# Attention scores in two pairs of PSUM banks, read by one exponential per pair, and two banks instead of three for the max pass

## The chip, the core and the metric

The program runs on one core of one Trainium2 chip. The metric is the device time of one execution in microseconds, from the first to the last instruction; the median of several executions is compared. The core has five engines with queues of their own: TensorE (PE in the profile, with its weight loads as PEld), VectorE (DVE), ScalarE (ACT), GpSimd (POOL) and SyncE (SP, which here only issues DMAs). They meet through semaphores. PSUM, where TensorE writes its results, has eight banks of 512 fp32 values per partition.

## What is computed

A macaron transformer block over 8 sequences of 1024 tokens with 256 channels: half a mixture-of-experts feed-forward, attention, and another half of the same feed-forward. The change lies in the attention alone, with 16 heads of 16 channels.

```python
x = x + 0.5 * ffn(layernorm(x))          # 8 experts, each 1024 tokens at most
x = x + attention(layernorm(x))
x = x + 0.5 * ffn(layernorm(x))

def attention(x):                         # B, T, C = 8, 1024, 256; H, D = 16, 16
    q, k, v = rope(heads(Wq, bq)), rope(heads(Wk, bk)), heads(Wv, bv)
    att = einsum('bhqd,bhkd->bhqk', q, k) / sqrt(D)
    att = softmax(where(causal, att, NEG_BIG), axis=-1)
    return einsum('bhqk,bhkd->bhqd', att, v) @ Wp.T + bp
```

## The kernel before

Attention works in 32 groups, each four heads of one sequence. Every engine runs the same loop over the groups, three groups in one turn of a hardware loop, and the last eight written out. While the scores of a group are worked on, the row maxima of the next group are made (the max pass, a first product of q and k), and q, k and v of a later group are projected and rotated (names with `prep`, `xt`, `qk`, `rot`, `part`). The last six groups have no such preparation beside them.

A group has 12 steps, numbered t = 0 to 11 here. A step is one tile of 128 keys against one half (512 columns) of the queries, for four heads; the columns left by the causal mask are 512, or 128, 256 and 384 at steps 1 to 3 and 5 to 7. TensorE's order within a step is written out in `body` in four shares c = 0 to 3: scores of heads 0 and 1 of the **next** step, a share of the max pass, scores of heads 2 and 3 of the next step, a share of the max pass, `times_v` of **this** step (probabilities times v), and the last two shares of the max pass. Pieces of the preparation come first in some shares.

The scores of a head go into one of `BANKS` = 3 banks `score_ps` in turn; ScalarE reads one bank with one exponential (`exponentials`, line 1356) and writes `probs`. A score product therefore waits (line 1467) until the exponential three heads earlier is done: the fourth head of a step waits for the exponential of the first head of the same step. On steps whose tile lies on the diagonal a second small product (line 1472) adds the mask.

The max pass is a ring of 50 places per group, called R0 to R49 here: 48 products (line 1457) and two transposes of finished maxima (line 1451; `SECOND` is R7, `FIRST` is R23). The products go into `max_ps`, also `BANKS` = 3 banks in turn. VectorE reads a bank (lines 1235 and 1238, the copy of line 1226 for a transpose) and counts `max_used`; TensorE's product of place r waits (line 1456) until place r - 3 was read. VectorE's order is written out as well: between its reads of the ring stand pieces of the preparation, such as `add_ffn` (line 1153), `leave` (1208), `xt_low` (1187) and `add_bias_qk` (1194). The maxima go by a DMA to DRAM and back into the q tile (`move_peaks`, issued by SyncE after the loads of a later group), and the first scores of the next group wait for that (line 1465).

Before the loop, the whole ring of group 0 and the head of the ring of group 1 run alone (lines 1507 to 1516).

Of the kernel before, what the change touches and what calls it, by code (L numbers as in the profile page):

```python
# [22 lines left out]
P = 128  # L23
# [12 lines left out]
GH = 4  # L36
# [6 lines left out]
ROWS_M = ROWS + PARTS  # L43
VW = 2 * D
SLOTS = 3
BANKS = 3
STEPS = [(0, j) for j in (0, 3, 2, 1)] + [(1, j) for j in (0, 7, 6, 5, 4, 1, 2, 3)]
NS = len(STEPS)
HALF = S // 2
# [779 lines left out]
def attention_block(nc, sh, dr):  # L829
# [6 lines left out]
    with ExitStack() as ctx:  # L836
        def sb(n, shape, dt):
            return ctx.enter_context(nc.sbuf_tensor(f"at_{n}", shape, dt))

        def ps(n, shape, dt=F32):  # L840
            return ctx.enter_context(nc.psum_tensor(f"at_{n}", shape, dt))
# [7 lines left out]
        probs = [sb(f"probs{k}", [P, GH, HALF], F32) for k in range(2)]  # L849
# [7 lines left out]
        hide_bf = sb("hide_bf", [P, P], BF16)  # L857
        junk = [sb(f"junk{k}", [P, HALF], F32) for k in range(BANKS)]
        y_in = [sb(f"y_in{k}", [P, C], F32) for k in range(2)]
# [21 lines left out]
        peak_t = sb("peak_t", [PARTS * GH * TPB // 2, P], BF16)  # L881
        o_out = [sb(f"o_out{k}", [P, HALF], F32) for k in range(2)]

        score_ps = [ps(f"score_ps{k}", [P, HALF]) for k in range(BANKS)]
        max_ps = [ps(f"max_ps{k}", [P, HALF]) for k in range(BANKS)]
        o_ps = ps("o_ps", [P, HALF])
        prep_ps = ps("prep_ps", [P, 2 * C])
# [34 lines left out]
        score_ready = sem("score_ready")  # L922
        exp_done = sem("exp_done")
# [42 lines left out]
        def bank(k, r):  # L966

            return place(k, r) % BANKS

# [4 lines left out]
        def _(sp):  # L974
# [28 lines left out]
            def move_peaks(g, u, half):  # L1003

                at = place(g, RING.index(FIRST)) if half == 0 else place(g + 1, RING.index(SECOND))
                wait_apart(sp, max_used, at + BANKS + 1, sh.passed)
                sp.dma_start(dr["peaks"][half].rearrange("a (r c) -> (a r) c", c=P), peak_t[:]
# [134 lines left out]
        def _(dve):  # L1142
# [97 lines left out]
            def split_peaks(g, half, stage):  # L1240

                at = (3 + 4) * g + 3 * half
                if stage == 0:
                    dve.wait_ge(max_used, (place(g, RING.index((1, 0))) if half == 0 else place(g + 1, 0)) + BANKS)
                else:
# [80 lines left out]
        @block.scalar  # L1326
        def _(act):
            a = nc.scalar

            def xt_high(n):  # L1330
                act.wait_ge(xt_ps_ready, n + 1)
                act.wait_ge(qk_ps_ready, 2 * n)
                a.copy(xt_hi[:].rearrange("p s c t -> p (s c t)"), prep_ps[:]).then_inc(xt_hi_ready, 1)

            def first_parts(n, s):
                act.wait_ge(rt_ps_ready, 2 * n + s + 1)
                act.wait_ge(stored, 16 * PAIR_STORES * n)
                a.copy(part[0][:, :, s * P:(s + 1) * P], prep_ps[:].rearrange("p (c t) -> p c t", t=P)
                       ).then_inc(part0_ready, 1)

            def second_parts(n, s):
                act.wait_ge(rest_ready, 2 * n + s + 1)
                a.copy(part[1][:, :, s * P:(s + 1) * P], rest[s][:]).then_inc(part1_ready, 1)

            def copy_o(g, half):
                act.wait_ge(pv_done, NS * g + LAST_STEP[half] + 3)
                act.wait_ge(o_stored[half], 16 * g)
                a.copy(o_out[half][:], o_ps[:]).then_inc(o_copied, 1)

            def exponentials(g, t):  # L1350

                c0, w, _ = columns(STEPS[t])
                act.wait_ge(pv_done, NS * g + t + 1)
                for h in range(GH):
                    act.wait_ge(score_ready, GH * (NS * g + t) + h + 1)
                    a.activation(probs[t % 2][:, h, c0:c0 + w], score_ps[(GH * t + h) % BANKS][:, 0:w],  # L1356
                                 ACT.Exp, scale=float(SCALE)).then_inc(exp_done, 1)

            act.sem_inc(exp_done, BANKS)
            act.sem_inc(o_copied, 1)  # L1360
            act.wait_ge(c_loaded, 16 * 10)
            a.copy(w_hi[:], w_raw).then_inc(w_hi_ready, 1)
            with act.Fori(0, LEAD - 1) as n:
                xt_high(n)
                for s in range(2):
                    first_parts(n, s)
                    second_parts(n, s)
            xt_high(LEAD - 1)
            exponentials(0, 0)

            def body(g, k, more, prepare, finish):
                n = g + LEAD
                for t in range(NS):
                    if t > 0:
                        exponentials(g, t)
                    if t == LAST_STEP[0] + 1:
                        copy_o(g, 0)
                    if finish:
                        if t == 1:
                            first_parts(n - 1, 0)  # L1380
                        if t == 3:
                            second_parts(n - 1, 0)
                            first_parts(n - 1, 1)
                        if t == 5:
                            second_parts(n - 1, 1)
                    if prepare and t == 5:
                        xt_high(n)
                if more:
                    exponentials(g + 1, 0)
                copy_o(g, 1)  # L1390

            groups(act, body)

        @block.tensor
        def _(pe):
# [64 lines left out]
            def scores(g, u, t, pr):  # L1460

                c0, w, diagonal = columns(STEPS[t])
                hf, j = STEPS[t]
                if t in FIRST_STEP.values() and pr == 0:
                    pe.wait_ge(peak_loaded[hf], 16 * (g + 1))
                for h in range(2 * pr, 2 * pr + 2):
                    pe.wait_ge(exp_done, GH * (NS * g + t) + h + 1)
                    out = score_ps[(GH * t + h) % BANKS]
                    last = te.matmul(out[:, 0:w], kk[u][:, h, j * P:(j + 1) * P],  # L1469
                                     q[u][:, h, hf * HALF + c0:hf * HALF + c0 + w], start=True, stop=not diagonal)  # L1470
                    if diagonal:
                        last = te.matmul(out[:, 0:P], sh.ident_bf[:], hide_bf[:], start=False, stop=True)  # L1472
                    last.then_inc(score_ready, 1)

            def times_v(g, u, t):
                c0, w, _ = columns(STEPS[t])
                hf, j = STEPS[t]
                pe.wait_ge(exp_done, GH * (NS * g + t + 1) + BANKS)
                if t == FIRST_STEP[hf]:
                    pe.wait_ge(o_copied, 2 * g + hf + 1)  # L1480
                for h in range(GH):
                    last = te.matmul(o_ps[h * VW:(h + 1) * VW, c0:c0 + w], vv[u][:, j, h, :],  # L1482
                                     probs[t % 2][:, h, c0:c0 + w], start=(t == FIRST_STEP[hf]),
                                     stop=(t == LAST_STEP[hf]), tile_position=(0, h * VW))
                last.then_inc(pv_done, 1)
# [233 lines left out]
```

## Time and profile before

| | us |
|---|---|
| median of 3 executions | 3192.55 |
| lowest and highest | 3189.92, 3194.87 |
| span of the profiled execution | 3194.8 |
| of that, attention's steps (first to last score product) | 829.7 to 2275 |
| TensorE busy, whole span | 2273.9 |
| VectorE busy, whole span | 1817.7 |
| ScalarE busy, whole span | 1234.8 |

The profiled execution has the span 3194.8 us; its own time is taken as the highest of the three, 3194.87. "Busy" of an engine is the time in which one of its instructions ran, by the profile's records. An engine that is not busy waits for a semaphore, or for its own sequencer. The steps of the attention fill 45% of the span; the two feed-forwards, the routing and the final gather fill the rest and share no instruction with the change.

### The profile page before, as it was taken

The numbers are of one execution on the slowest core, as the hardware profiler recorded it, in microseconds if no ns is written. First come the engines' busy times: TensorE is split into PE (matmuls) and PEld (weight loads), VectorE is DVE, ScalarE is ACT, GpSimd is POOL, SyncE is SP. The second block draws the span as 40 slices with busy tenths as digits, with TensorE's granted clock in tenths as the row PEclk, the third lists the DMA queues.
The fourth block names the chain that finished last, engine by engine and source line by source line (L and its number), as shares of the span: only waits on it lengthen the run. The fifth ranks groups of instructions, "written<-read, shape, count | busy, mean of one in ns | idle before, by whom it ended". The sixth has DMA issues, their size and how long they took to land. (4 is left out here: it accounts for less than half of the span.)

```text
span 3194.8 us, 53878 instructions
## 1 busy us (share of the span) xinstructions
PE 2273.9 (71%) x14405; PEld 1452.4 (45%) x14405; DVE 1817.7 (57%) x5300; ACT 1234.8 (39%) x2626; POOL 800.4 (25%) x1308
## 2 busy tenths in 40 slices
PE   4508999934887788888887878889455506999910
PEld 4407888823333333333333333323145406888810
DVE  4535554343776766777676777767366634544412
ACT  1104555411354445545454545556411103555400
POOL 2250000056132323333232333200134260000044
PEclk9999999955798999999898999999767657999955
DMA  5023223025243543443443534543222023232133
GB/s 213 23 87 126 85 81 99 27 67 115 51 97 76 98 94 73 104 94 83 95 90 76 104 86 81 100 82 75 76 85 79 4 94 118 82 99 90 35 99 118
DMA packets 227705, 276.33 MB, mean 86 GB/s; under 512 B 22401, under 2 KB 172801, under 8 KB 226433
## 3 DMA queue, kind: packets, MB, share of 16 engines
q1 hardware_dynamic: 215168, 239.77, 30.1%
q0 software_dynamic: 12288, 33.57, 3.4%
q8 instruction: 117, 1.92, 0.3%
q14 instruction: 132, 1.07, 0.1%
HBM read 162.90 MB, written 110.36 MB: 86 GB/s over the span
## 5 line engine op out<-in xcount | busy, mean ns | idle before, releaser
L1356 ACT ACTIVATE at_probs<-at_score_ps 128x512 f32<-128x512 f32 (+3 forms) x1536 | 650.0, 494 | 575.0 <-PE at_score_ps L1472 435.2
L1235 DVE CUSTOM_DVE_ANT_0 at_junk<-at_max_ps,at_causal 128x128 f32<-128x128 f32 (+3 forms) x1024 | 490.9, 486 | 250.3 <-PE at_max_ps L1457 241.7
L1469 PE MATMUL at_score_ps<-at_q,at_k 99*128 99x512 bf16 (+3 forms) x1536 | 452.1, 341 | 90.4 <-ACT at_probs L1356 41.4
L1457 PE MATMUL at_max_ps<-at_k,at_q 96*128 96x512 bf16 (+3 forms) x1536 | 461.0, 344 | 28.5 <-DVE at_peak L1235 20.8
L1238 DVE TENSOR_REDUCE at_peak<-at_max_ps 128x1 f32<-128x512 f32 x512 | 352.4, 688 | 146.4 <-PE at_max_ps L1457 145.1
L710 DVE TENSOR_TENSOR f_hid_lo<-f_hid,f_hid_hi 128x512 fp32r<-128x512 f32 x256 | 177.2, 692 | 348.4 <-ACT f_hid_hi L748 347.4
L1482 PE MATMUL at_o_ps<-at_probs,at_v 128*32 128x512 f32 (+3 forms) x3072 | 347.4, 526 | 4.7 <-issue 4.6
L1457 PEld LDWEIGHTS at_max_ps<-at_k,at_q 96*128 96x128 bf16 x1536 | 130.2, 99 | 374.6 <-DVE at_peak L1235 179.5
L794 PE MATMUL f_y_ps<-f_w_hi,f_hid_hi 128*128 128x256 f32 x1024 | 291.1, 284 | 2.9 <-issue 0.2
L794 PE MATMUL f_y_ps<-f_w_hi,f_hid_lo 128*128 128x256 f32 x1024 | 290.1, 283 | 0.0
L794 PE MATMUL f_y_ps<-f_w_lo,f_hid_hi 128*128 128x256 f32 x1024 | 289.4, 283 | 0.0
L745 ACT ACTIVATE f_hid<-f_hid_ps 128x512 f32<-128x512 f32 x256 | 153.3, 599 | 334.5 <-PE f_hid_ps L780 332.6
L1469 PEld LDWEIGHTS at_score_ps<-at_q,at_k 99*128 99x128 bf16 x1536 | 146.4, 101 | 259.8 <-ACT at_probs L1356 144.9
L1472 PE MATMUL at_score_ps<-at_hide_bf,ident_bf 128*128 128x128 bf16 x1024 | 224.2, 231 | 0.0
L1084 POOL TENSOR_TENSOR at_by_cos<-at_qk,at_cos 128x512 f32<-128x512 f32 x64 | 81.5, 1274 | 512.5 <-DVE at_qk L1194 511.0
L794 PEld LDWEIGHTS f_y_ps<-f_w_hi,f_hid_hi 128*128 128x128 f32 x1024 | 194.6, 190 | 24.3 <-issue 15.2
L769 PE MATMUL f_xt_ps<-ident,f_xe 128*128 128x128 f32 x256 | 39.8, 282 | 226.4 <-DMA f_xe<-expert_in 226.4
L794 PEld LDWEIGHTS f_y_ps<-f_w_lo,f_hid_hi 128*128 128x128 f32 x1024 | 194.7, 190 | 8.8
L794 PEld LDWEIGHTS f_y_ps<-f_w_hi,f_hid_lo 128*128 128x128 f32 x1024 | 194.9, 190 | 0.0
L780 PE MATMUL f_hid_ps<-f_xt_hi,f_w_hi 128*128 128x512 f32 x512 | 167.9, 409 | 18.2 <-DVE f_w_lo L687 18.2
L748 ACT CAST f_hid_hi<-f_hid 128x512 fp32r<-128x512 f32 x256 | 158.6, 620 | 8.1
L780 PE MATMUL f_hid_ps<-f_xt_lo,f_w_hi 128*128 128x512 f32 x512 | 161.4, 396 | 0.0
(144 smaller groups left out, 3746.4 us busy)
## 6 DMA issues: line engine op xcount, KB each, us to landing
f_w_raw<-in_w SPq DMA_DIRECT2D x32, 1024.0 KB, 6.7
qk<-at_part SPq DMA_DIRECT2D x96, 256.0 KB, 2.7
at_q<-qk SPq DMA_DIRECT2D x192, 128.0 KB, 4.4
at_k<-qk SPq DMA_DIRECT2D x192, 128.0 KB, 7.0
f_xe<-expert_in SPq DMA_DIRECT2D x32, 512.0 KB, 6.3
expert_out<-f_y SPq DMA_DIRECT2D x32, 512.0 KB, 3.0
v_rows<-at_v_out SPq DMA_DIRECT2D x64, 256.0 KB, 3.1
at_v<-v_rows SPq DMA_DIRECT2D x32, 512.0 KB, 8.8
```

Of the source, the lines that this page charges most:

```text
L710: v.tensor_tensor(hid_lo[f % NHID][:], hid[f % NHID][:], hid_hi[f % NHID][:].bitcast(F32), ALU.subtract).then_inc(hid_lo_ready, 1)
L745: nc.scalar.activation(hid[f % NHID][:], hid_ps[f % 2][:], ACT.Gelu_apprx_tanh).then_inc(hid_ready, 1)
L748: nc.scalar.copy(hid_hi[f % NHID][:], hid[f % NHID][:]).then_inc(hid_hi_ready, 1)
L780: last = nc.tensor.matmul(hid_ps[f % 2][:], w[ws][:, cc, f * P:(f + 1) * P], x[k][:, cc, :], start=(i == 0), stop=(i == 3 * CC - 1))
L794: last = nc.tensor.matmul(y_ps[t][:], a[m][:, rows], w[ws][:, f, :], start=(f == 0 and i == 0), stop=(f == FC - 1 and i == 2))
L1235: v.tensor_tensor_reduce(junk[bank(k, r)][:, 0:w], src, causal[:, HALF - w:HALF], 1.0, LEAST, ALU.add, ALU.max, out).then_inc(max_used, 1)
L1238: v.tensor_reduce(out, src, AX.X, ALU.max).then_inc(max_used, 1)
L1356: a.activation(probs[t % 2][:, h, c0:c0 + w], score_ps[(GH * t + h) % BANKS][:, 0:w], ACT.Exp, scale=float(SCALE)).then_inc(exp_done, 1)
L1457: te.matmul(max_ps[bank(u, r)][:, 0:w], q[u][0:ROWS, h, i * P:(i + 1) * P], kk[u][0:ROWS, h, k0:k0 + w], start=True, stop=True).then_inc(m ...
L1469: last = te.matmul(out[:, 0:w], kk[u][:, h, j * P:(j + 1) * P], q[u][:, h, hf * HALF + c0:hf * HALF + c0 + w], start=True, stop=not diagonal)
L1472: last = te.matmul(out[:, 0:P], sh.ident_bf[:], hide_bf[:], start=False, stop=True)
L1482: last = te.matmul(o_ps[h * VW:(h + 1) * VW, c0:c0 + w], vv[u][:, j, h, :], probs[t % 2][:, h, c0:c0 + w], start=(t == FIRST_STEP[hf]), st ...
```

## The change

The three score banks become two tiles of two banks each, heads 0 and 1 in `score_ps[0]`, heads 2 and 3 in `score_ps[1]`. One exponential reads both banks of a pair, so ScalarE runs 2 exponentials for a step in place of 4, and `exp_done` counts pairs. TensorE waits once for a pair, before its first head, until the exponential two pairs earlier is done, which is the same pair of the step before. `BANKS` becomes 2, which after this change sizes the max pass alone (`max_ps`, and the scratch tiles `junk`). PSUM holds 4 + 2 + 1 + 1 banks, before 3 + 3 + 1 + 1.

```diff
-BANKS = 3
+BANKS = 2
+PAIR_BANKS = 2
...
-        score_ps = [ps(f"score_ps{k}", [P, HALF]) for k in range(BANKS)]
+        score_ps = [ps(f"score_ps{k}", [P, 2, HALF]) for k in range(PAIR_BANKS)]
         max_ps = [ps(f"max_ps{k}", [P, HALF]) for k in range(BANKS)]
...
                 act.wait_ge(pv_done, NS * g + t + 1)
-                for h in range(GH):
-                    act.wait_ge(score_ready, GH * (NS * g + t) + h + 1)
-                    a.activation(probs[t % 2][:, h, c0:c0 + w], score_ps[(GH * t + h) % BANKS][:, 0:w],
+                for pr in range(2):
+                    act.wait_ge(score_ready, GH * (NS * g + t) + 2 * pr + 2)
+                    a.activation(probs[t % 2][:, 2 * pr:2 * pr + 2, c0:c0 + w], score_ps[pr][:, :, 0:w],
                                  ACT.Exp, scale=float(SCALE)).then_inc(exp_done, 1)
 
-            act.sem_inc(exp_done, BANKS)
+            act.sem_inc(exp_done, PAIR_BANKS)
...
+                pe.wait_ge(exp_done, 2 * (NS * g + t) + pr + 1)
                 for h in range(2 * pr, 2 * pr + 2):
-                    pe.wait_ge(exp_done, GH * (NS * g + t) + h + 1)
-                    out = score_ps[(GH * t + h) % BANKS]
+                    out = score_ps[pr][:, h % 2, :]
...
-                pe.wait_ge(exp_done, GH * (NS * g + t + 1) + BANKS)
+                pe.wait_ge(exp_done, 2 * (NS * g + t + 1) + PAIR_BANKS)
```

On ScalarE, two steps of a group (384 and then 512 columns) in the program before; `score_ps0` to `score_ps2` are the three banks.

```order
L1355 ISA [waits at_pv_done]
L1356 ACTIVATE at_probs1<-at_score_ps1 128x384 [waits at_score_ready]
L1355 REGISTER_ALU
L1356 ACTIVATE at_probs1<-at_score_ps2 128x384 [waits at_score_ready]
L1355 REGISTER_ALU
L1356 ACTIVATE at_probs1<-at_score_ps0 128x384 [waits at_score_ready]
L1355 REGISTER_ALU
L1356 ACTIVATE at_probs1<-at_score_ps1 128x384 [waits at_score_ready]
```

The same place of the program after the change (its line numbers are one higher); `score_ps0` and `score_ps1` are now the pairs.

```order
L1356 ISA [waits at_pv_done]
L1357 ACTIVATE at_probs1<-at_score_ps0 128x2x384 [waits at_score_ready]
L1356 REGISTER_ALU
L1357 ACTIVATE at_probs1<-at_score_ps1 128x2x384 [waits at_score_ready]
L1354 REGISTER_ALU
```

Four reads of one bank have become two reads of two banks, with half the waits. On TensorE, the scores of step 8 (512 columns with the mask, made during step 7) with the max products between them, before:

```order
L1472 MATMUL at_score_ps0<-at_hide_bf,ident_bf 128x128
L1456 REGISTER_ALU
L1457 MATMUL at_max_ps0<-at_k1,at_q1 128x512 [waits at_max_used]
L1467 REGISTER_ALU
L1469 MATMUL at_score_ps1<-at_q0,at_k0 128x512 [waits at_exp_done]
L1472 MATMUL at_score_ps1<-at_hide_bf,ident_bf 128x128
L1467 REGISTER_ALU
L1469 MATMUL at_score_ps2<-at_q0,at_k0 128x512 [waits at_exp_done]
L1472 MATMUL at_score_ps2<-at_hide_bf,ident_bf 128x128
L1456 REGISTER_ALU
L1457 MATMUL at_max_ps1<-at_k1,at_q1 128x384 [waits at_max_used]
```

And after:

```order
L1473 MATMUL at_score_ps0<-at_hide_bf,ident_bf 128x128
L1457 REGISTER_ALU
L1458 MATMUL at_max_ps0<-at_k1,at_q1 128x512 [waits at_max_used]
L1467 REGISTER_ALU
L1470 MATMUL at_score_ps1<-at_q0,at_k0 128x512 [waits at_exp_done]
L1473 MATMUL at_score_ps1<-at_hide_bf,ident_bf 128x128
L1470 MATMUL at_score_ps1<-at_q0,at_k0 128x512
L1473 MATMUL at_score_ps1<-at_hide_bf,ident_bf 128x128
L1457 REGISTER_ALU
L1458 MATMUL at_max_ps1<-at_k1,at_q1 128x384 [waits at_max_used]
```

The order of the products is the same. The last head of a step has lost its own wait for `exp_done`, and the two max products around it now use bank 0 and bank 1 of two, where they used bank 0 and 1 of three.

## Rows read from the trace of the kernel before

**Rows 1.** The page's head: span, and busy time of each engine.

```profile
span 3194.8 us, 53878 instructions
...
PE 2273.9 (71%) x14405; PEld 1452.4 (45%) x14405; DVE 1817.7 (57%) x5300; ACT 1234.8 (39%) x2626; POOL 800.4 (25%) x1308
```

**Rows 2.** Stretches: length, busy PE, PEld, DVE, ACT, POOL, PE clock, DMA.

```profile
1100.00:2100.00 1000.00, 824.75 (x5483) 360.84 (x5481) 707.15 (x2288) 505.67 (x1156) 309.69 (x506) 0.94 0.43 90
802.00:830.00 28.00, 25.07 (x60) 6.20 (x60) 26.75 (x107) 0.00 (x0) 4.13 (x4) 0.50 0.00 1
...
1503.10:1514.70 11.60, 9.16 (x69) 4.03 (x67) 11.01 (x40) 7.52 (x18) 4.53 (x6) 1.00 0.15 50
...
2120.00:2275.00 155.00, 143.25 (x1043) 51.00 (x1041) 100.47 (x350) 100.65 (x241) 0.00 (x0) 1.00 0.29 60
```

**Rows 3.** Waits in 1100 to 2100: us in total, times, longest.

```profile
DVE at_junk L1235 <- PE at_max_ps L1457: 169.8, 152, 6.1
PEld at_max_ps L1457 <- DVE at_peak L1235: 114.2, 139, 1.7
...
PEld at_score_ps L1469 <- ACT at_probs L1356: 87.1, 186, 1.3
...
PE at_max_ps L1451 <- DVE at_peak_part L1259: 35.3, 22, 2.0
...
PE at_score_ps L1469 <- ACT at_probs L1356: 26.5, 47, 1.0
PE at_score_ps L1469 <- DMA at_q<-peaks: 25.0, 12, 4.0
```

**Rows 4.** Groups by form in 1000 to 2200: count, busy us, mean ns, idle before.

```profile
L1356 ACT ACTIVATE at_probs<-at_score_ps 128x512 f32<-128x512 f32 x624 | 327.5, 602 | 251.7 <-PE at_score_ps L1472 134.3 <-PE at_score_ps L1469 116.4
```

**Rows 5.** Timeline, steps 3 and 4 of one group: start, us, instruction, [idle before].

```profile
1503.35 1.64 ACT L1356 ACTIVATE at_probs<-at_score_ps 128x384 f32<-128x384 f32 x4 [0.62 <-PE at_score_ps L1472]
...
1503.55 0.22 PE L1472 MATMUL at_score_ps<-at_hide_bf,ident_bf 128*128 128x128 bf16 x1
...
1503.90 0.34 PE L1469 MATMUL at_score_ps<-at_q,at_k 99*128 99x384 bf16 x1
...
1506.80 2.07 ACT L1356 ACTIVATE at_probs<-at_score_ps 128x512 f32<-128x512 f32 x4
...
1507.45 0.39 PE L1469 MATMUL at_score_ps<-at_q,at_k 99*128 99x512 bf16 x1 [0.96 <-ACT at_probs L1356]
```

**Rows 6.** Timeline, step 4 of the same group: R17 on VectorE, R19 on TensorE.

```profile
1510.87 0.69 DVE L1238 TENSOR_REDUCE at_peak<-at_max_ps 128x1 f32<-128x512 f32 x1
...
1511.01 0.39 PE L1457 MATMUL at_max_ps<-at_k,at_q 96*128 96x512 bf16 x1 [0.83 <-DVE at_peak L1235]
```

**Rows 7.** Timeline, steps 5 and 6: R24, R25, R26, and the projection's wait.

```profile
1515.13 0.43 PE L1457 MATMUL at_max_ps<-at_k,at_q 96*128 96x512 bf16 x2
...
1515.66 0.69 DVE L1238 TENSOR_REDUCE at_peak<-at_max_ps 128x1 f32<-128x512 f32 x1 [0.79 <-PE at_max_ps L1457]
...
1516.27 0.28 DVE L1235 CUSTOM_DVE_ANT_0 at_junk<-at_max_ps,at_causal 128x128 f32<-128x128 f32 x1
...
1516.47 0.69 DVE L1238 TENSOR_REDUCE at_peak<-at_max_ps 128x1 f32<-128x512 f32 x1
...
1518.02 0.68 DVE L1187 TENSOR_TENSOR at_xt_lo<-at_prep_ps,at_xt_hi 128x512 fp32r<-128x512 f32 x1
...
1518.75 0.73 PE L1412 MATMUL at_prep_ps<-at_w_hi,at_xt_hi 128*128 128x512 f32 x2 [1.19 <-DVE at_xt_lo L1187]
```

**Rows 8.** Timeline, step 9: R40 on VectorE, R42 on TensorE.

```profile
1529.65 0.69 DVE L1238 TENSOR_REDUCE at_peak<-at_max_ps 128x1 f32<-128x512 f32 x1 [0.71 <-PE at_max_ps L1457]
...
1529.93 0.38 PE L1457 MATMUL at_max_ps<-at_k,at_q 96*128 96x512 bf16 x1
```

**Rows 9.** Timeline: a max product in the ring ahead of the loop.

```profile
813.63 0.63 PE L1457 MATMUL at_max_ps<-at_k,at_q 96*128 96x512 bf16 x1
```

**Rows 10.** Waits in 2120 to 2275, the groups without preparation.

```profile
PEld at_score_ps L1469 <- ACT at_probs L1356: 31.6, 64, 0.8
```

## The prediction, made before the changed kernel ran

> **What bounds the kernel now.** I read the page first: TensorE is busy 71% of the span, VectorE 57%, ScalarE 39% [rows 1]. These are means over stages, and the change touches one: the stretch table for 1100 to 2100, the middle of attention, has TensorE 82% busy, VectorE 71%, ScalarE 51% [rows 2]. No engine is full, yet nothing else holds them up for long: TensorE and VectorE pass the max ring to and fro and wait for each other by turns. The list of waits shows it [rows 3]: VectorE waits for max products 169.8 us in that millisecond, TensorE's weight loads for freed max banks 114.2 us. TensorE's waits for exponentials come next: 87.1 us on the weight loads, 26.5 us on the products. The weight-load figure counts time in which a product still runs, the other leaves short gaps out, so the true loss lies between: 38 to 126 us over the 1447 us of attention.
>
> The timeline of one group shows both at work. Step 3: the third head's mask starts at 1503.55 and the fourth head's scores only at 1503.90, once the exponential that began at 1503.35 is over; a product after a small mask otherwise follows within 0.06 us, so 0.3 us is lost [rows 5]. Step 4 loses 1.1 us: ScalarE comes late from two casts and starts at 1506.80 [rows 5]. But from 1503.1 to 1514.7 VectorE is busy 11.01 of 11.6 us [rows 2]: it has the routed rows' sum, layernorm statistics and splits to do beside the ring. There TensorE's time is worth nothing until VectorE's list is done, and at 1511.01 it waits 0.83 us for a bank anyway [rows 6].
>
> **What the change removes.** 768 of 1536 exponentials. Four in a row at 512 columns take 2.07 us and one alone 0.60 [rows 4, 5], so they start (2.07 - 0.60)/3 = 0.49 us apart; the columns cost about 0.43 of it, if the step from the 384-column row (1.64 for four) to the 512-column row (2.07) is read as slope: 0.43/4 = 0.107 per 128 columns. That leaves 0.06 us for each exponential removed, 46 us of ScalarE, which is 49% idle in attention: nothing of it reaches the end. The Trainium skill (ScalarE: Activation LUTs, "What ACT_TABLE_LOAD costs") gives 186 ns + 0.833 ns per column for such an instruction, with 93 ns of it under the next one; by that the saving would be 93 ns each and 71 us of ScalarE. Here the rows give less, and neither enters the sum.
>
> The removed wait is worth more. A pair waits for the same pair of the step before, whose exponential was done long ago (ScalarE stands idle before each step's first, [rows 4]). So the fourth head's stall goes everywhere: 0.3 us on most diagonal steps, 1.1 us at step 4. Starting a pair's exponential only after the second head costs 0.2 us of start, regained at the end (two of 1.03 us against four); times_v comes two shares of the ring later and is not reached.
>
> **What it adds: a shorter ring.** TensorE may write place r only when r - 2 is read. From the rows: what VectorE hands over lets TensorE start 0.05 us later (xt_low ends at 1518.02 + 0.68 = 1518.70, the projection starts at 1518.75), and a 512-column product is in VectorE's hands 0.53 us after its start (1515.13 to 1515.66, [rows 7]). VectorE spaces its reads 0.61 us at 512 columns and 0.20 at 128 [rows 7]. If TensorE waits, a place is served 0.59 us after r - 2 was freed; meanwhile VectorE has only r - 1 to read. Behind a 128-column place it then idles 0.4 us, behind 256 or 384 columns 0.3 or 0.2, behind 512 about 0.05.
>
> Walking through the group of the rows:
> - Steps 0 to 2, VectorE has slack: the removed stall at step 2 brings R11 and the start of VectorE's busy stretch forward, **-0.3**.
> - Steps 3 to 5, VectorE is the bound. The 0.3 and 1.1 us are swallowed. R19, which had to wait for R16, now waits for R17: read until 1510.87 + 0.69 = 1511.56, so it starts at 1511.61 instead of 1511.01 [rows 6]. VectorE loses 0.3 behind the 128-column R18; the transposes of step 5 wait for R22 and slip as well, which leaves 0.14 at R24.
> - R26 must now wait for R24 (its read at 1516.47, less 0.53, says that it started before 1515.94, and R24 was read until 1516.35, [rows 7]): VectorE idles 0.44 behind R25, then 0.3 behind R27. xt_low ends 0.14 + 0.44 + 0.3 later, and the projection, which waited 1.19 us for it [rows 7], with it: **+0.9**.
> - Steps 6 to 10, TensorE is the bound again. R42 waits for R40: 1529.65 + 0.69 + 0.05 = 1530.39 instead of 1529.93, 0.46 us [rows 8]. I count two such places and one stall of 0.3 saved: **+0.6**.
> - These make 1.2 us by the next group's first score, which waits for the maxima by DMA, 12 times in that millisecond (of about 21 groups), 2.1 us each and 4.0 in this group, the longest [rows 3]. Such a wait hides the 1.2. The DMAs' chain starts after leave at step 4, whose time moves +0.3 - 0.3 = 0. I let half of the 1.2 through: **+0.6** on average.
> - Step 11 and step 0: R3 waits for R1, R7 (the transpose) for R5, +0.4, less 0.2 of stalls at steps 0 and 1; TensorE stood before that transpose anyway (35.3 us, 22 times, [rows 3]): **+0.2**.
>
> A group thus grows by 0.6 + 0.2 = **0.8 us**, the 26 groups with preparation by 21 us.
>
> The ring ahead of the loop (802 to 830) has VectorE busy 26.75 of 28 us at half clock [rows 2], where a 512-column product takes 0.63 us instead of the 0.38 to 0.39 of the full clock [rows 6, 8, 9], so a bank's round is longer by 0.24, about 0.83 us. Each of the 16 places behind a narrow one loses 0.5, the others 0.1 to 0.4; with what the splits of the maxima fill, **+15 us** once. The last six groups are TensorE's (143 of 155 us busy, [rows 2]), with 31.6 us of weight-load waits for exponentials in 155 [rows 10]; VectorE has slack, but wide places without projections between them cost 0.2 us a step. I take **-1 us** each, -6. The clock is 0.94 in the middle [rows 2], so 12% of the time is at its lower level (1.2 of 2.4 GHz), after the long stops; shorter stops at a group's first score may spare a tenth of that, **-6**.
>
> Sum: 21 + 15 - 6 - 6 = +24 us on the profiled execution's 3194.9; it stands 2.3 us above the median of the three, 3192.6, so **3217 us**, 0.8% slower. The parts of the program outside attention don't change.
>
> **Rivals.**
> - *Faster: the stalls' gain passes.* The score stalls add up to about 80 us over attention (between 38 and 126, above). If VectorE's busy stretch starts earlier whenever TensorE is earlier, and the ring costs no more than 30, the time is 3192.6 - 50 = 3143. For it: in the last six groups this must be so. Against: the largest single stall lies in VectorE's busy stretch. It decides where the idle of VectorE before its ring reads shrinks instead of grows.
> - *No change.* The DMA of the maxima sets the period in more than half of the groups; if in nearly all, both effects vanish in its wait: 3192.
> - *Much slower: the ring's waits add up.* 139 waits for a bank in 1000 us [rows 3]; each grows by up to one read, 0.6 us: 83 us, over attention 120: 3312. Against: waits in a row share one delay, and the transposes' and xt_low's waits absorb.
> - *Slower by the wide exponential.* If banks come free too late because one instruction of 1.03 us holds two, TensorE stalls before the third head instead of the fourth. It would need an exponential of the step before that ends after the next scores; only step 4's is so late, and there the next step's third head would wait 0.1 us or more: with the ring's cost, 3192.6 + 24 + 32 x 0.5 = 3233. The Trainium skill (Perfetto Trace Analysis, "Optimizing Scalar/DVE Operations") says that where ScalarE isn't full but causes gaps on others, instructions should be broken up, not merged. By that rule this case would hold; the rows show the gap at the fourth head alone, which the fourth bank takes away.
>
> **How the numbers follow.** A measurement of this kernel tells 0.2% (6 us) from nothing. Forecast, +7 to +60 us: 0.50. Ring's waits add up: 0.08. Wide exponential: 0.06. No change: 0.13. Faster: 0.23. The range for eight in ten, 3150 to 3262, leaves out the deeper part of the faster case and the ring's adding up. The forecast's own range is 3199 to 3253. Faster by over 0.2%: 0.23; within: 0.13; slower: 0.64.
>
> **What would show it.** In the changed kernel's profile: waits of score products for exponentials near zero; waits of max products for VectorE clearly up, above 160 us per millisecond on the weight loads; the stretch from the first max product to the first score longer by some 15 us; exponentials of 1024 columns at 1.03 us; R26 starting after R24 was read; waits for the maxima's DMA down. I am wrong if the last six groups' gain is found in the groups with preparation too, or if a group grows by more than 2 us.

## The result, and the profile of the changed kernel

The changed kernel takes 3346.72 us (median of 4 runs, 3346.67 to 3348.75) against 3193.71 us for the kernel before (4 runs, 3189.92 to 3198.52). The ratio is 1.0475, with a 95% interval of [1.0461, 1.0490]: 153 us slower, where 24 were forecast.

The page of the changed kernel: the span, the busy times, and the granted clock in 40 slices of the span.

```profile
span 3346.9 us, 51958 instructions
...
PE 2416.8 (72%) x14405; PEld 1507.9 (45%) x14405; DVE 1854.8 (55%) x5300; ACT 1193.1 (36%) x1858; POOL 798.3 (24%) x1308
...
PEclk9999999755787878878887888898966756999965
```

Beside [rows 1], ScalarE has 768 instructions fewer and 41.7 us less work (46 were forecast). TensorE runs the same 14405 products, yet is busy 143 us longer. A product of 512 columns takes 0.38 or 0.39 us at the higher clock and 0.61 to 0.63 at the lower in these traces, and the clock row says where the lower one stands: sevens and eights through attention. The stretch table shows it in full: first the millisecond of [rows 2], then attention cut at the first transpose read of the fourth group and at that 22 groups later.

```profile
1100.00:2100.00 1000.00, 842.53 (x4946) 365.89 (x4948) 662.82 (x2077) 430.02 (x586) 293.12 (x494) 0.83 0.39 82
...
839.60:999.00 159.40, 137.07 (x795) 59.01 (x794) 106.15 (x333) 71.66 (x96) 44.78 (x77) 0.82 0.37 79
999.00:2166.00 1167.00, 984.57 (x5765) 426.67 (x5766) 773.49 (x2419) 502.50 (x682) 337.90 (x569) 0.83 0.39 81
2166.00:2428.60 262.60, 226.79 (x1545) 86.00 (x1544) 164.06 (x544) 138.16 (x187) 15.04 (x15) 0.93 0.33 66
```

The millisecond holds 4946 products where it held 5483, at a granted clock of 0.83 where it was 0.94. The clock has two levels, 1 and 0.5 in these rows (2.4 and 1.2 GHz), so 34% of the time is at the lower one, before 12%. The same 22 groups in the kernel before:

```profile
972.00:2029.60 1057.60, 868.02 (x5767) 382.60 (x5768) 748.96 (x2419) 530.30 (x1210) 338.88 (x568) 0.94 0.43 90
2029.60:2275.00 245.40, 217.23 (x1545) 80.77 (x1542) 158.24 (x546) 148.39 (x352) 15.23 (x15) 0.97 0.35 71
```

One copy of the finished maxima (`FIRST`) stands in each group, so its first and last start give the length of a mean group. The tile views of the changed kernel (count, durations in ns, first and last start), for the 22 groups, then the six after them, then the whole of attention:

```profile
L1227 DVE COPY at_peak_t<-at_max_ps x45: 215/217/219, 998.7 to 2166.1; 48x128 bf16<-48x128 bf16 x45
...
L1227 DVE COPY at_peak_t<-at_max_ps x13: 215/217/218, 2166.1 to 2409.9; 48x128 bf16<-48x128 bf16 x13
...
L1470 PE MATMUL at_score_ps<-at_q,at_k x1536: 218/379/634, 839.6 to 2428.6; 99*128 99x512 bf16 x128, 99*128 99x256 bf16 x64
...
L1458 PE MATMUL at_max_ps<-at_k,at_q x1536: 217/380/650, 801.3 to 2406.7; 96*128 96x512 bf16 x128, 96*128 96x128 bf16 x32, 96*128 96x384 bf16 x32
```

And the kernel before:

```profile
L1226 DVE COPY at_peak_t<-at_max_ps x45: 210/217/220, 971.9 to 2029.6; 48x128 bf16<-48x128 bf16 x45
...
L1226 DVE COPY at_peak_t<-at_max_ps x13: 208/210/217, 2029.6 to 2253.4; 48x128 bf16<-48x128 bf16 x13
...
L1457 PE MATMUL at_max_ps<-at_k,at_q x1536: 217/379/634, 802.2 to 2250.2; 96*128 96x512 bf16 x128, 96*128 96x128 bf16 x32, 96*128 96x384 bf16 x32
```

A mean group with preparation was (2029.6 - 971.9)/22 = 48.1 us and is (2166.1 - 998.7)/22 = 53.1. The last score started at 2274.9 and starts at 2428.6, 153.7 later. That splits into 9.9 for the first score (829.7 to 839.6), 16.9 up to the fourth group, 109.7 in the 22 groups and 17.2 behind them.

The waits in 1100 to 2100, for [rows 3], and the widest exponential, for [rows 4]:

```profile
PEld at_max_ps L1458 <- DVE at_peak L1236: 182.3, 263, 1.9
DVE at_peak L1239 <- PE at_max_ps L1458: 151.3, 223, 2.4
DVE at_junk L1236 <- PE at_max_ps L1458: 149.7, 150, 6.1
PEld at_max_ps L1458 <- DVE at_peak L1239: 124.2, 150, 1.7
...
PE at_max_ps L1458 <- DVE at_peak L1236: 59.5, 94, 1.2
...
PE at_max_ps L1458 <- DVE at_peak L1239: 26.1, 68, 0.8
...
PE at_score_ps L1470 <- DMA at_q<-peaks: 1.4, 1, 1.4
```

```profile
L1357 ACT ACTIVATE at_probs<-at_score_ps 128x1024 f32<-128x1024 f32 x272 | 275.9, 1025 | 255.1 <-PE at_score_ps L1473 132.9 <-PE at_score_ps L1470 117.6
```

The waits of scores for exponentials are gone from the list: 87.1 and 26.5 us became nothing on either. The waits for the maxima's DMA fell from 25.0 us to 1.4. In their place TensorE's products wait 86 us for VectorE (before 18), its weight loads 306 (before 162). The 18 and the 162 need these rows of the kernel before beside [rows 3]:

```profile
PEld at_max_ps L1457 <- DVE at_peak L1238: 47.3, 83, 0.8
...
PE at_max_ps L1457 <- DVE at_peak L1235: 14.5, 18, 0.8
...
PE at_max_ps L1457 <- DVE at_peak L1238: 3.4, 21, 0.2
```

So the prediction's sign "above 160 us per millisecond on the weight loads" told little: the prediction counted 114.2, the waits for line 1235 alone, and both lines together had 162 before. The waits moved the way that was forecast, and the time did not.

One group shows the rest. TensorE's timeline from step 3 on, those products alone that waited (R16, R17, R18, R19, R24, R26 and the projection behind xt_low):

```profile
1544.59 0.39 PE L1458 MATMUL at_max_ps<-at_k,at_q 96*128 96x512 bf16 x1 [1.21 <-DVE at_peak L1236]
...
1545.73 0.39 PE L1458 MATMUL at_max_ps<-at_k,at_q 96*128 96x512 bf16 x1 [0.52 <-DVE at_peak L1236]
...
1546.79 0.27 PE L1458 MATMUL at_max_ps<-at_k,at_q 96*128 96x128 bf16 x1 [0.44 <-DVE at_peak L1236]
1547.39 0.61 PE L1458 MATMUL at_max_ps<-at_k,at_q 96*128 96x512 bf16 x1 [0.34 <-issue]
...
1554.88 0.82 PE L1458 MATMUL at_max_ps<-at_k,at_q 96*128 96x512 bf16 x2 [0.20 <-DVE at_peak L1239]
...
1556.39 0.61 PE L1458 MATMUL at_max_ps<-at_k,at_q 96*128 96x512 bf16 x1 [0.69 <-DVE at_peak L1239]
...
1558.49 1.22 PE L1413 MATMUL at_prep_ps<-at_w_hi,at_xt_hi 128*128 128x512 f32 x2 [0.43 <-DVE at_xt_lo L1188]
```

At 1546.79 a 128-column product still takes 0.27 us, at 1547.39 a 512-column one takes 0.61 and no longer 0.39. VectorE, doing `add_ffn` and the statistics, hands over a bank late three times in a row; TensorE has no written-ahead place left and stops three times, and then its clock halves. By stretches of 1 us, 16 of the 22 groups have such a stretch of 16 or 17 us at the lower level; the kernel before has none over 13 us.

VectorE's own work grew too, by 24.5 us in the 22 groups for the same 2419 instructions. Most of that is one small instruction, the add of line 1260 (line 1259 before): 16 columns, two in each group. In the group shown it starts at 1550.49 and takes 0.86 us, beside GpSimd's `at_part` from 1550.17 to 1551.32; its shortest takes 0.17. Over the 22 groups it takes 40.6 us, in the kernel before 25.9.

### The profile page after: what moved, and what is told of

Its sections match the earlier page's. It is cut to its first block and busy times, and to the rows that moved or that the text cites. A ratio compares the mean times of both kernels' runs of the same rounds, so it can differ in the third digit from the quotient of the medians.

```text
span 3346.9 us, 51958 instructions
## 1 busy us (share of the span) xinstructions
PE 2416.8 (72%) x14405; PEld 1507.9 (45%) x14405; DVE 1854.8 (55%) x5300; ACT 1193.1 (36%) x1858; POOL 798.3 (24%) x1308
## 5 line engine op out<-in xcount | busy, mean ns | idle before, releaser
L1357 ACT ACTIVATE at_probs<-at_score_ps 128x1024 f32<-128x1024 f32 (+3 forms) x768 | 609.4, 811 | 735.0 <-PE at_score_ps L1473 572.3
L1458 PE MATMUL at_max_ps<-at_k,at_q 96*128 96x512 bf16 (+3 forms) x1536 | 520.4, 374 | 167.0 <-DVE at_peak L1236 91.4
L1470 PE MATMUL at_score_ps<-at_q,at_k 99*128 99x512 bf16 (+3 forms) x1536 | 444.8, 356 | 9.8 <-issue 5.8
L1458 PEld LDWEIGHTS at_max_ps<-at_k,at_q 96*128 96x128 bf16 x1536 | 142.0, 103 | 642.2 <-DVE at_peak L1236 305.2
L1483 PE MATMUL at_o_ps<-at_probs,at_v 128*32 128x512 f32 (+3 forms) x3072 | 382.9, 568 | 0.6 <-ACT at_probs L1357 0.4
```

The source lines that it names most:

```text
L1357: a.activation(probs[t % 2][:, 2 * pr:2 * pr + 2, c0:c0 + w], score_ps[pr][:, :, 0:w], ACT.Exp, scale=float(SCALE)).then_inc(exp_done, 1)
L1458: te.matmul(max_ps[bank(u, r)][:, 0:w], q[u][0:ROWS, h, i * P:(i + 1) * P], kk[u][0:ROWS, h, k0:k0 + w], start=True, stop=True).then_inc(m ...
```

## The experiments

Two theories stood after the result. **The clock**: TensorE's stops in VectorE's busy stretch make the clock fall there in almost every group, and most of the 153 us is work at 1.2 GHz. **The ring**: the waits themselves add up, and the clock only follows. A third, **the wide exponential**, was still open from the prediction. Each ratio below is to the kernel before on the same chip, with its 95% interval.

### The two halves of the change apart

`ring2` gives the max pass two banks and leaves scores and exponentials as before. `score4` adds to it a fourth single score bank, so it differs from the changed kernel by one exponential for each bank alone.

```diff
-BANKS = 3
+BANKS = 2
+SCORE_BANKS = 3        # ring2;  4 in score4
-        score_ps = [ps(f"score_ps{k}", [P, HALF]) for k in range(BANKS)]
+        score_ps = [ps(f"score_ps{k}", [P, HALF]) for k in range(SCORE_BANKS)]
```

> Edit: the max pass gets two banks, the scores keep their three single banks and four exponentials per step; one PSUM bank stays unused. Theory K (clock): the two-bank ring lets TensorE stand so long at steps 3 to 6 that its clock falls to the lower level in every group, and the slow stretch that follows is most of the loss; then this kernel is at least as slow as the changed one (3347), 3340 to 3400, with the low clock in every group. Theory W (waits alone): the ring's waits add up by themselves, the clock adds little; the kernel is also slow, about 3347 plus the 40 to 80 us that the fourth head's stalls cost, 3390 to 3430. Rival M (merging): the wide exponentials or the pair's waits are the loss, and the ring costs only the 24 us of the forecast: 3210 to 3230.

> Edit: as the changed kernel in banks (four for scores, two for the max pass), but four single score banks with an exponential and a wait each. It differs from the changed kernel in the merging alone. Theories K and W: within 10 us of 3347, since ScalarE has slack either way. Rival M: well below 3347, near 3220.

Measured: ring2 3307.50 us, 1.0383 [1.0354, 1.0411]; score4 3310.62 us, 1.0403 [1.0377, 1.0429]. Most of the loss is in the shorter ring alone. No theory's number came for ring2: it is 32 us under the clock theory's range, 82 under that of the waits and 77 above the third's. score4 is 36 us under the 3347 that both theories gave it. The stretch tables for 1100 to 2100, ring2 and then score4:

```profile
1100.00:2100.00 1000.00, 820.02 (x5042) 358.76 (x5042) 666.98 (x2127) 469.50 (x1062) 297.53 (x507) 0.89 0.39 84
```

```profile
1100.00:2100.00 1000.00, 842.93 (x4978) 368.67 (x4978) 662.93 (x2091) 465.34 (x1046) 294.30 (x494) 0.83 0.39 82
```

The fourth bank takes the stalls on exponentials away and earns nothing: the clock falls from 0.89 to 0.83. Against the changed kernel, score4 is 0.7 points better: its interval ends at 1.0429, those of the changed kernel begin at 1.0461 and, in `after_again` below, at 1.0431. But they ran on different chips. In score4 a mean group is 52.6 us, in the changed kernel 53.1; the six groups behind take 235.1 us (2144.9 to 2380.0) against 243.8, with a clock of 0.96 against 0.92. So the wide exponential as such may cost about 0.7%, which no run on one chip settles, and it brings hardly a stall of scores: over all of attention the products wait for it 1.9 us, 4 times.

### Keeping the clock up with products that nobody reads

`after_fill` is the changed kernel with 19 more products of 512 columns in each group with preparation, written into a score bank that is free at that moment, just ahead of the max places where TensorE stood waiting. They change no result and use none of the max banks. `ring2_fill` does the same to ring2, in the spare eighth bank. `before_fill` puts 11 such products into the kernel before, ahead of its two longest stops (R7, and the group's first score); they go into the bank that is written next.

```diff
+FILL = {16: 4, 17: 3, 18: 2, 19: 2, 22: 3, 26: 2, 28: 3}     # place: products ahead of it
...
+    if prepare and r in FILL:
+        step, pr = (t + 1, 1) if c == 0 else (t + 2, 0)
+        pe.wait_ge(exp_done, 2 * (NS * g + step) + pr + 1)
+        for _ in range(FILL[r]):
+            te.matmul(score_ps[pr][:, 0, :], q[k][0:ROWS, 0, 0:P], kk[k][0:ROWS, 0, 0:HALF], ...)
     ring(ahead, u, r)
```

> Edit: two banks for the max pass, three single score banks, and in the free bank products of 512 columns that nobody reads, issued just ahead of the ring places at which TensorE stands (4 before R16, 3 before R17, 2 before R18 and R19, 3 before R22, 2 before R26, 3 before R28), 19 in a group, 4.1 us of extra TensorE work per group in the groups with preparation. Theory K: the clock stays up and the kernel is faster than the two-bank kernel without fillers by 60 to 150 us, in spite of the work. Theory W: the fillers lie in waits or cost up to 4.1 us in each of 26 groups: the same or up to 100 us slower.

> Edit to the changed kernel: 19 products of 512 columns per group that nobody reads, into score banks that are free at that moment, ahead of the ring places at which TensorE stands in steps 3 to 5 (groups with preparation only). Theory K (clock): the clock stays at its upper level through steps 5 and 6, a group shortens by about 4 us, the kernel by 80 to 110 us, to 1.013 to 1.022 of the kernel before. Theory W (waits alone): the same time or slower, 1.045 or more.

> Edit to the kernel before: 6 unread products ahead of the wait of the second transpose (R7, where TensorE stands 1.9 us in each group) and 5 ahead of the wait for the maxima at a group's first score (1.1 us, hidden in the DMA wait of more than half of the groups). Low clock is 123 us in the middle millisecond here. If these two stops are what lets it fall, it gains 20 to 50 us; if the loop's turn or the longer DMA waits do, it gains nothing or loses up to 20.

> The changed kernel unaltered, as the yardstick on the chip of the three kernels beside it. Expected: 1.045 to 1.05 of the kernel before, with 17 us of low clock in most groups of attention.

Measured: after_again (the changed kernel once more, on this chip) 3347.72 us, 1.0473 [1.0431, 1.0516]. after_fill 3249.67 us, 1.0169 [1.0129, 1.0210]: more work on TensorE, and 98 us faster. ring2_fill 3266.25 us, 1.0255 [1.0229, 1.0282], 41 us faster than ring2, where 60 to 150 were forecast. before_fill 3216.09 us, 1.0055 [1.0030, 1.0079]: its clock in 1100 to 2100 rises from 0.94 to 0.96, and the kernel before still loses 16 us by it.

The same place of the same group in three kernels, by the stretch table: 5.8 us around `add_ffn`, from the same two score products of 512 columns on, and the 17 us behind. After, after_fill, before:

```profile
1541.10:1546.90 5.80, 3.62 (x28) 1.71 (x26) 5.50 (x19) 3.95 (x7) 3.37 (x5) 1.00 0.15 36
1546.90:1563.90 17.00, 15.23 (x65) 6.21 (x65) 8.96 (x28) 4.00 (x6) 3.82 (x14) 0.50 0.75 159
```

```profile
1485.90:1491.70 5.80, 5.62 (x37) 2.22 (x36) 5.50 (x19) 4.01 (x7) 3.32 (x5) 1.00 0.16 41
1491.70:1508.70 17.00, 15.51 (x104) 7.18 (x105) 12.23 (x38) 5.85 (x8) 4.89 (x15) 1.00 0.75 165
```

```profile
1460.80:1466.60 5.80, 3.93 (x29) 1.68 (x27) 5.50 (x19) 4.18 (x11) 3.46 (x5) 1.00 0.17 51
1466.60:1483.60 17.00, 14.81 (x107) 7.31 (x110) 12.44 (x39) 7.56 (x17) 6.54 (x17) 1.00 0.78 160
```

Compare the second rows. In the same 17 us the changed kernel gets 65 products through, its filled version 104, the kernel before 107. VectorE's share shows whose fault it is not: 8.96 us busy against 12.23. Compare the first rows too: 3.62 of 5.80 us busy was followed by the lower clock, 3.93 of 5.80 was not. The changed kernel and the kernel before are close to each other there; what exactly tips it these rows don't tell.

after_fill over the 22 groups, by the stretch table and by the tile view of the transposes:

```profile
986.00:2064.00 1078.00, 956.87 (x6184) 417.34 (x6185) 757.57 (x2421) 498.40 (x682) 338.14 (x569) 0.95 0.42 88
```

```profile
L1228 DVE COPY at_peak_t<-at_max_ps x45: 216/217/218, 986.1 to 2064.0; 48x128 bf16<-48x128 bf16 x45
...
L1228 DVE COPY at_peak_t<-at_max_ps x13: 212/217/218, 2064.0 to 2303.0; 48x128 bf16<-48x128 bf16 x13
```

A mean group is 49.0 us there at a clock of 0.95. With 48.1 before and 53.1 in the changed kernel, the fillers give back 4.1 us of the 5.0, and 0.9 are left for the two banks' own waits together with what the fillers themselves cost. Not all of the 4.1 need be the clock: line 1260's add is back at 26.2 us in the 22 groups, 14.4 less than in the changed kernel, and no run shows how much of that reached the end. Its list of waits, though, still shows 255 us of waits for max banks on the weight loads in 1100 to 2100 (306 in the changed kernel, 162 before):

```profile
PEld at_max_ps L1459 <- DVE at_peak L1237: 145.0, 286, 1.4
...
PEld at_max_ps L1459 <- DVE at_peak L1240: 110.2, 180, 0.8
```

For the changed kernel this decides between the two theories: the waits are there, and most of the time is gone. For ring2 it doesn't: with its clock raised from 0.89 to 0.96 it is still 85 of its 126 us above the kernel before. Its waits of scores for exponentials (38.8 us over attention) and the fillers' own work are in those 85, and no run takes them apart.

### Giving VectorE less to do at once

The other way to take the stops out is to move VectorE's work. `spread_after` and `spread_before` put the six pieces of `add_ffn` at steps 6 to 8 in place of steps 2 to 4, and GpSimd's gather and inverse roots behind them.

```diff
+ADD_AT = {(6, 0): 0, (6, 2): 1, (7, 2): 2, (7, 3): 3, (8, 0): 4, (8, 2): 5}
...
-                            stage = SHARES * (t - 2) + c - 1
-                            if 0 <= stage < 6 and (...):
+                            stage = ADD_AT.get((t, c))
+                            if stage is not None and (...):
...
-                        if t == 4 and (...):            # gather
+                        if t == 7 and (...):
```

> Edit to the kernel before: VectorE's sum of routed rows and layernorm statistics (3.5 us per group) leave steps 2 and 3 for steps 6 to 8, where VectorE stands idle, and GpSimd's gather and Newton steps follow to steps 7 and 9 to 11. If VectorE's busy stretch at steps 2 to 6 is what bounds that part, as the prediction says, the kernel gains 1 to 3 us in each of 26 groups: 3120 to 3170. If the ring is bound by the round trip anywhere, nothing changes: 3185 to 3200.

> Edit to the changed kernel: VectorE's sum of routed rows and layernorm statistics go from steps 2 and 3 to steps 6 to 8, GpSimd's gather and Newton steps to steps 7 and 9 to 11. Theory K: TensorE no longer stands 1.3 us before R16 and 0.7 before R17 and R18, which are what lets the clock fall; the clock stays up in most groups and the kernel gains 60 to 110 us. Theory W: the alternation of wide and narrow places from R17 on costs the same as before, the gain is below 30 us.

Measured: spread_before 3172.66 us, 0.9986 [0.9963, 1.0010]; spread_after 3238.42 us, 1.0133 [1.0092, 1.0174]. The same move is worth nothing with three banks and 109 us with two. The 1 to 3 us a group that spread_before was to gain if VectorE's stretch is the bound did not come. No product was added here, so it is not the unread products as such that helped. The clock of spread_after in 1100 to 2100:

```profile
1100.00:2100.00 1000.00, 841.04 (x5387) 372.02 (x5384) 697.23 (x2250) 461.36 (x634) 310.92 (x521) 0.92 0.43 90
```

### Grouping the ring by width

In the ring's second half wide and narrow places alternate (512 columns, then 128 to 512). With two banks VectorE has only the narrow one to read while the next wide one is made. `grouped_after` orders each row block as four wide places and then four narrow ones; `grouped_before_b` does it with three banks, `spread_grouped_after` together with the spread work.

```diff
-        for h in range(GH):
-            w = (i + 1) * P
...
-                out += [(h, i, 0, HALF, False), (h, i, HALF, w - HALF, True)]
+            out += [(h, i, 0, HALF, False) for h in range(GH)]
+            out += [(h, i, HALF, w - HALF, True) for h in range(GH)]
```

> Edit to the changed kernel: in the second half of the ring the four 512-column places of a row block come first, then its four narrow ones, instead of wide and narrow in turn. With two banks VectorE idles about 0.4 us behind each narrow place that a wide one follows, and 0.05 behind a wide one. Expected if that alternation is what makes steps 4 to 6 long: the ring ahead of the loop shortens from 38 to about 33 us, the groups without preparation by 1 to 2 us each, and the others by that and by what the clock then gives back: 1.02 to 1.035 of the kernel before. If only the number of banks matters, not the order: 1.045 or more.

> Edit: both moves on the changed kernel, VectorE's list spread and the ring's places grouped. The spread alone gave 1.013. If the two are independent, the alternation's 1 to 2 us per group come off as well: 0.995 to 1.005 of the kernel before, perhaps faster than it.

> The order of the ring's second half by width (four wide places, then four narrow ones), on the kernel before with its three banks. Theory: the grouping helps the changed kernel because two banks leave VectorE idle behind a narrow place that stands between two wide ones; with three banks the place behind a narrow one was already written, so the grouping has little to give: ratio to the kernel before 0.990 to 1.003, a mean group with preparation 47.3 to 48.3 us (48.1 before), the last six groups within 2 us of their 224. Rival: the alternation costs with any number of banks (VectorE's four narrow reads in a row are short of work for TensorE's products anyway), and the grouping is worth as much here as in the changed kernel: ratio about 0.97 (100 us off), a mean group below 46 us, the last six groups 13 us shorter.

Measured: grouped_after 3248.73 us, 1.0174 [1.0147, 1.0201], 3.0 points of the ratio (some 96 us) better than the changed kernel and a little better than forecast. grouped_before_b 3185.63 us, 1.0027 [1.0009, 1.0045]: with three banks the order by width gives nothing. Its last six groups took 223.6 us, as forecast; its mean group of (2035.5 - 963.5)/22 = 48.7 us was 0.4 above the theory's bound. spread_grouped_after 3190.89 us, 0.9978 [0.9963, 0.9993]: with both orders changed, two max banks do as well as three in the old orders (three banks with both changed were not run). grouped_after's stretches, 1100 to 2100 and the six groups at the end, and the transposes there:

```profile
1100.00:2100.00 1000.00, 837.66 (x5339) 369.41 (x5336) 703.18 (x2224) 458.34 (x629) 308.50 (x517) 0.91 0.42 88
2072.00:2301.00 229.00, 201.90 (x1405) 78.09 (x1406) 164.44 (x544) 122.60 (x166) 14.86 (x14) 0.96 0.36 73
```

```profile
L1227 DVE COPY at_peak_t<-at_max_ps x13: 216/217/218, 2071.9 to 2300.6; 48x128 bf16<-48x128 bf16 x13
```

The last six groups take 228.7 us, against 243.8 in the changed kernel, 239.0 in after_fill and 223.8 before. There the alternation of widths is 10 to 15 of the 20 us.

grouped_before_b shows one thing more. The 22 groups of it, and those of ring2:

```profile
963.50:2035.50 1072.00, 913.14 (x5768) 397.66 (x5769) 766.14 (x2423) 531.35 (x1210) 339.00 (x569) 0.88 0.42 89
```

```profile
983.20:2128.40 1145.20, 942.36 (x5766) 412.23 (x5767) 760.62 (x2420) 537.16 (x1210) 337.95 (x569) 0.88 0.39 83
```

Both have a clock of 0.88 and the same work, on different chips, and ring2 takes 73 us longer. The kernel before, at 0.94, takes 1057.7 us, only 14 less than grouped_before_b. So the mean clock does not tell the time by itself, and ring2's loss is not the clock's alone. Whether the lower level costs little where it stands in grouped_before_b, or the new order gained what it cost, no run shows.

### Three banks, with the one long stall removed

`spread_act` starts from the kernel before: the spread work, and on ScalarE the casts (`first_parts`) that made step 4's exponentials 1.1 us late are put behind that step's first exponential.

```diff
                                  ACT.Exp, scale=float(SCALE)).then_inc(exp_done, 1)
+                    if h == 0 and after_first is not None:
+                        after_first()
```

> Edit to the kernel before (three banks each): VectorE's list spread, and ScalarE's cast of step 3 moved behind the first exponential of step 4, so that the fourth head's stall of 1.1 us at step 4 shrinks to about 0.4. The spread alone gave 0.9986. With VectorE no longer the bound there the 0.7 us should pass: 0.990 to 0.997. If VectorE still bounds steps 3 to 5: 0.998.

Measured: 3169.30 us, 0.9910 [0.9887, 0.9932], as forecast and the lowest ratio of all, with one bank for each exponential and three for the max pass, at a clock of 0.91 in 1100 to 2100. Of its waits in 1100 to 2100, the score products' for exponentials (before 26.5 us, longest 1.0):

```profile
PE at_score_ps L1471 <- ACT at_probs L1357: 13.2, 46, 0.3
```

## Why the prediction was right in direction and wrong in size

**The step that failed is the clock term.** The prediction wrote that "shorter stops at a group's first score may spare a tenth of that, -6". The stops at the first score did shrink (25.0 to 1.4 us of waits), but the clock's low time did not follow them. It moved to the steps where VectorE is the bound, and grew there: 34% of the 22 groups where it had been 12%. after_fill puts a number to it: 1167.4 - 1077.9 = 89 us in these 22 groups, 4.1 us each, and 101 us from the first score to the end of them. The fillers' own work makes that number too small, line 1260's add may make it up to 14 us too large. A group grew by 5.0 us in all, where the prediction called itself wrong above 2. What hid it was the sentence that in VectorE's busy stretch TensorE's time "is worth nothing until VectorE's list is done". For the end of that stretch that is true; for the clock that TensorE has behind it, it is not.

**Where the stops are.** The walk said that R19 would be the one to wait, for R17. In the changed kernel R16, R17 and R18 wait already (1.21, 0.52 and 0.44 us in the group shown), and R19 starts 0.34 us after them without a wait for VectorE in the list: `add_ffn`'s two pieces stand between two reads, and one place less is written ahead of them. In the 5.8 us shown TensorE is busy 3.62 us where it was 3.93, but the time comes as several stops close together.

**The group's +0.8.** Near, once the clock is held: +0.9 (48.1 to 49.0) with the fillers in it. That it came so near is in part luck, two misses that cancel. The share that the DMA's wait hides was too small, and the waits behind it as well: in after_fill 4.9 us of that wait are left of 25.0, so by this estimate it hid 20.1/21 = 1.0 us a group where I let it hide 0.6, and without it the group would have grown by 1.9, not 1.4. That the removed stalls at steps 3 and 4 are worth nothing is not shown apart: score4 takes all of them away and is no faster than ring2, but its clock is lower too.

**The ring ahead of the loop.** +15 was forecast; from the first max product to the first score it is 27.5 us before (802.2 to 829.7) and 38.3 after (801.3 to 839.6), +10.8. The direction holds, the price of a narrow place doesn't: grouped_after, where in the second half of the ring a wide place follows a narrow one only once in each row block, still takes 36.2 us (800.6 to 836.8), 2.1 less and not the 5 that were expected. What makes up the rest stays open.

**The last six groups.** -6 was forecast, +20 came (223.8 to 243.8). The wait of weight loads for exponentials, 31.6 us in 155, did go [rows 10]; but I counted the ring's cost there only between wide places (0.2 us a step) and not behind the narrow ones, as I had done for the ring ahead of the loop. grouped_after bears that term out with 10 to 15 of the 20. Some of the 20 is the clock again (0.92 over them, before 0.97 over a stretch that is nearly the same).

**Rivals.** *The ring's waits add up* came nearest in time (3312), but not by its mechanism: with the clock held up the weight loads still wait 255 us a millisecond for max banks, and the group grows by 0.9. *The wide exponential*: the stall before the third head that it needed is not there; about 0.7% is left between one exponential and two, measured on different chips and with a lower clock in the last six groups beside it, and no run separates these. The Trainium skill's rule (Perfetto Trace Analysis, "Optimizing Scalar/DVE Operations"), to break instructions up where they cause gaps on others, points the same way as that remainder, but the gap it speaks of doesn't show. *Faster* and *no change* fell: the DMA's wait could hide a little, not 5 us a group.

In sum, with the first score at 838.8 in after_fill: up to the end of the 22 groups, what the fillers give back is 101 us (12 in the first groups and 89 in the 22), what the two banks keep is 25 (5 and 20); the first score comes 10 us later, and 17 are added behind the 22 groups. That makes the trace's 153.7. The 101 are named after the clock by the experiments above; the 17 are not taken apart fully.

## What to carry to other kernels

When a change moves an engine's waiting, ask where its pauses will stand, not only whether they lie beside other work: pauses of TensorE inside another engine's bound may cost nothing there, and much behind. Read the granted clock by stretches of a few microseconds before and after, and put a price on both levels; in the changed kernel it was the largest term by far, while grouped_before_b had as much of the lower level as ring2 and was not slowed like it. A ring of banks between two engines should be judged by the work that the reader does between two reads, and by the order of wide and narrow places: with both put right, two banks did what three had done in the old orders.

## What the runs showed of the hardware

The clock's behaviour was not what I expected in four ways. More work made a kernel faster: 19 unread products a group, 0.38 us each by their records, took 98 us off. The clock fell without a long stop: in the group shown none in the 20 us before was over 1.21 us, and TensorE was busy 3.62 of the 5.80 us before, yet it then ran 17 us at 1.2 GHz. And TensorE reads as *busier* when it is slow (842.5 us of the millisecond for 4946 products, before 824.8 for 5483), so its busy share alone would have pointed the wrong way. The price of the lower level was well under its half: in the 22 groups the changed kernel has 0.34 x 1167 = 397 us of it and after_fill 0.10 x 1078 = 108, and the 289 us between them cost 89, or 0.31 us for each. This is an estimate for this pair alone: grouped_before_b has 0.24 x 1072 = 257 us of the lower level, the kernel before 0.12 x 1058 = 127, and their 22 groups differ by 14 us. VectorE's work beside it goes on at its own pace (a reduction of 512 columns takes 0.689 us in both kernels), but for the small add of line 1260: beside GpSimd's instruction it took 0.86 us and ended with it, where its shortest took 0.17.
